# Masking each bank of attention scores by itself, with mask tiles of 64 by 64, in an attention and expert kernel

## What is computed

```python
Q = x @ W_q + b_q; K = x @ W_k + b_k; V = x @ W_v + b_v
scores = jnp.einsum('bhqd,bhkd->bhqk', Qh, Kh)
scores = (scores + jnp.einsum('bhqd,qkd->bhqk', Qh, rel_k)) / scale
scores = jnp.where(causal[None, None], scores, -1000000000.0)
attn = jax.nn.softmax(scores, axis=-1)
out = jnp.einsum('bhqk,bhkd->bhqd', attn, Vh) + jnp.einsum('bhqk,qkd->bhqd', attn, rel_v)
x = x + _layernorm(out @ W_o + b_o)
x = x + _layernorm(ffn(_layernorm(x)))
```

## Time and profile before

| what | value |
|---|---|
| runs | 1043.07, 1037.00, 1040.29 us; median 1040.29 |
| the profiled execution | 1038.87 us, its span in the trace 1037.1 us |
| PE busy | 907.4 us, 87% |
| DVE busy | 834.9 us, 80% |
| POOL busy | 726.3 us, 70% |
| ACT busy | 678.6 us, 65% |
| mask products (L1537) | 1280 matmuls, 199.3 us recorded |
| score products for the maxima (L1516) | 1024 matmuls, 215.5 us |
| score products for the exponentials (L1493) | 1024 matmuls, 196.3 us |
| maxima on DVE (L1127) | 640, 409.3 us |

### The profile page before, as it was taken

One profiled execution on the slowest core, in us unless ns is written; L12 is line 12 of the kernel. 1 busy time (PEld: TensorE's weight loads), 2 busy tenths in 40 slices (PEclk: granted clock), 3 DMA queues, 4 the chain that ended last, 5 costly groups with the idle time before them and its releaser, 6 DMA issues. The chain is left out here.

```text
span 1037.1 us, 23478 instructions
## 1 busy us (share of the span) xinstructions
PE 907.4 (87%) x7655; PEld 519.9 (50%) x7655; DVE 834.9 (80%) x1948; ACT 678.6 (65%) x1305; POOL 726.3 (70%) x940
## 2 busy tenths in 40 slices
PE   2768899999999899999998999987679999999995
PEld 0324444444444444454444444432357777777773
DVE  5677878888888888888888888886568788878884
ACT  2137677767786777777867776765447767676763
POOL 4135676966867868668678686576257989898886
PEclk8569999999999999999999999998979999999999
DMA  2610111101101101011011010102415454554541
GB/s 50 168 45 28 37 39 34 51 33 41 46 32 45 43 33 48 31 43 47 32 45 43 32 49 32 42 13 57 149 58 169 143 165 151 171 148 167 162 139 31
DMA packets 64004, 74.93 MB, mean 72 GB/s; under 512 B 10032, under 2 KB 39600, under 8 KB 63904
## 3 DMA queue, kind: packets, MB, share of 16 engines
q1 hardware_dynamic: 61536, 73.17, 22.2%
q10 hardware_dynamic: 2368, 0.48, 0.3%
HBM read 43.75 MB, written 8.65 MB: 51 GB/s over the span
## 5 line engine op out<-in xcount | busy, mean ns | idle before, releaser
L1127 DVE TENSOR_REDUCE mx<-ps_s 128x1 f32<-128x512 f32 (+2 forms) x640 | 409.3, 684 | 82.3 <-PE ps_s L1537 80.5
L799 ACT ACTIVATE prob<-ps_e 128x512 f32<-128x512 f32 x640 | 347.8, 601 | 121.6 <-PE ps_e L1493 121.6
L640 POOL TENSOR_SCALAR_AFFINE_SELECT prob<-prob 128x516 f32<-128x516 f32 (+1 forms) x320 | 174.0, 568 | 171.3 <-ACT prob L799 171.3
L1516 PE MATMUL ps_s<-ks,qs 63*128 63x512 f16 (+3 forms) x1024 | 215.5, 311 | 20.6 <-DMA ks<-kl 8.6
L1493 PE MATMUL ps_e<-qs,ks 64*128 64x512 f16 (+3 forms) x1024 | 196.3, 304 | 15.8 <-DMA qs<-mT 7.8
L1553 PE MATMUL ps_av<-prob,vp 128*32 128x512 f32 (+3 forms) x2048 | 183.8, 455 | 22.7 <-POOL prob L640 22.4
L721 POOL TENSOR_TENSOR hidden_low<-hidden,hidden_high 128x512 fp32r<-128x512 f32 x144 | 191.2, 1356 | 12.1 <-ACT hidden_high L988 10.8
L1493 PEld LDWEIGHTS ps_e<-qs,ks 64*128 64x128 f16 x1024 | 60.9, 95 | 116.8 <-ACT prob L799 63.9
L988 ACT CAST hidden_high<-hidden 128x512 fp32r<-128x512 f32 x160 | 98.3, 614 | 30.4 <-DVE hidden L1440 25.8
L1537 PE MATMUL ps_s<-masked_at,below_r 64*128 64x130 bf16 (+3 forms) x640 | 106.5, 211 | 0.0
L1516 PEld LDWEIGHTS ps_s<-ks,qs 63*128 63x128 f16 x1024 | 63.6, 95 | 78.0 <-DVE mx L1127 54.5
(11 more groups left out here) (176 smaller groups left out, 1738.4 us busy)
## 6 DMA issues: line engine op xcount, KB each, us to landing
gate_rows<-gates_dram SPq DMA_DIRECT2D x128, 256.0 KB, 3.6
qs<-qh SPq DMA_DIRECT2D x128, 32.0 KB
qs<-ql SPq DMA_DIRECT2D x128, 32.0 KB
xnT_dram<-oT SPq DMA_DIRECT2D x16, 256.0 KB, 2.0
xeT<-xnT_dram SPq DMA_DIRECT2D x16, 256.0 KB, 2.7
out<-result SPq DMA_DIRECT2D x16, 256.0 KB, 2.3
v_near<-v_back SPq DMA_DIRECT2D x16, 254.0 KB
ks<-kh SPq DMA_DIRECT2D x124, 32.0 KB
```

What stands on the lines that cost most here:

```text
L640: pool.affine_select(out=v, in_=v, compare_op=ALU.is_ge, fill=0.0, base=-2, pattern=cols, channel_multiplier=-1).then_inc(S["p_masked"], 1)
L799: act.activation(prob[g % 2][:, u, b, :], ps_e[bank][:, :], ACT.Exp, scale=SCALE).then_inc(S["e_done"], 1)
L1127: dve.tensor_reduce(out, src, AX.X, ALU.max).then_inc(s_free[bank], 1)
L1516: pe.matmul(scores[:, at:at + P * (qt + 1)], qs[par][rows, 2 * g + off, P * qt:P * qt + P], ks[par][rows, 2 * g + off, 0:P * (qt + 1)], st ...
```

## The change

- `s_mask` replaces `diagonals` and `s_masks`. It masks one bank and one half of the queries: `part` chooses queries 0 to 63 or 64 to 127 of each block, and the weights are `below[rows, rows]`, 64 rows by 64 columns, a tile of 64 by 64. Part 1 moves 65 columns per block, as before; part 0 masks the rest and moves 129 columns for one block, 257 for two neighbouring ones and 258 for two of 256 keys. There are still two masks per bank and four per round. The half that must not be touched is masked at once for all of its keys, so `below_r` is not needed.
- `below_r` and `roll_halves` (two copies on ACT and a wait on PE) are gone. `masked_at` grows from 65 to 257 columns and is made by six selects on POOL instead of four.
- `exp_unit` and `s_unit` are cut into bank and part (`e_unit`, `e_part`), so that a round can alternate single products of the two halves. Each bank is masked, and signals `s_full`, when its own products are through: the upper one in the middle of the round, the lower one at the end.
- The number of instructions on PE stays the same. On PE the shape of consecutive tiles changes more often, as the order below shows.

The diff (whole):

```diff
--- before
+++ after
@@ -234,8 +234,7 @@
         ident = sb("ident", [P, P])
         ident16 = sb("ident16", [P, P], F16)
         below = sb("below", [P, P], BF16)
-        below_r = sb("below_r", [P, P], BF16)
-        masked_at = sb("masked_at", [P, HALF + 1], BF16)
+        masked_at = sb("masked_at", [P, 2 * P + 1], BF16)
         head_sel = sb("head_sel", [P, D, NPAIR, 2])
         head_sum = sb("head_sum", [P, 32])
         wq_in = sb("wq_in", [P, P])
@@ -378,7 +377,7 @@
 
 
         names = """
-            attn_loaded qk_loaded x_loaded0 x_loaded1 x_loaded2 const_made const_ready rolled bias_full bias_ready
+            attn_loaded qk_loaded x_loaded0 x_loaded1 x_loaded2 const_made const_ready bias_full bias_ready
             m_made masked_made v_rows k_rows q_rows
             dve_own pool_own gate_own dve_own2 pool_own2 passed_sp passed_pool passed_dve passed_pe
             s_full s_free0 s_free1 s_free2 e_full e_done misc_full misc_free
@@ -596,13 +595,17 @@
 
             def masked_columns():
 
-                for i, (base, columns) in enumerate(((0, slice(0, HALF)), (-HALF, slice(0, HALF)),
-                                                     (1 - HALF, slice(HALF, HALF + 1)), (1 - P, slice(HALF, HALF + 1)))):
-                    v = masked_at[:, columns]
-                    pool.affine_select(out=v, in_=v, compare_op=ALU.not_equal, fill=MASKED, base=base,
-                                       pattern=[[-1 if i < 2 else 0, v.shape[1]]],
-                                       channel_multiplier=1).then_inc(S["masked_made"], 1)
-                    pool.wait_ge(S["masked_made"], i + 1)
+                blocks = masked_at[:, 1:].rearrange("p (n c) -> p n c", n=2)
+                parts = ((masked_at[:, 0:1], 0, [[0, 1]]),
+                         (blocks[:, :, 0:HALF - 1], 1, [[0, 2], [-1, HALF - 1]]),
+                         (blocks[:, :, HALF - 1:], HALF - 1, [[0, 2], [0, HALF + 1]]))
+                made = 0
+                for v, row, pattern in parts:
+                    for b in range(2):
+                        pool.affine_select(out=v, in_=v, compare_op=ALU.not_equal, fill=MASKED, base=-row - HALF * b,
+                                           pattern=pattern, channel_multiplier=1).then_inc(S["masked_made"], 1)
+                        made += 1
+                        pool.wait_ge(S["masked_made"], made)
 
             def selectors():
 
@@ -782,12 +785,6 @@
                         act.dma_start(ks0[lo:lo + D, 0:NPAIR // 2, :],
                                       part[HALF * b:HALF * b + 32, :]).then_inc(stacks[0][0], 16)
 
-            def roll_halves():
-
-                act.wait_ge(S["const_ready"], N_POOL_CONST)
-                act.copy(below_r[0:HALF, :], below[HALF:P, :]).then_inc(S["rolled"], 1)
-                act.copy(below_r[HALF:P, :], below[0:HALF, :]).then_inc(S["rolled"], 1)
-
             def exp_unit(st, i):
                 g, u, b = i // (2 * NU), i % (2 * NU) // 2, i % 2
                 n, bank = st.e_use(f"e{i}")
@@ -906,8 +903,6 @@
                     act.wait_ge(S["gates_stored"], 32)
                     rest = (NSEQ - EARLY) * NE * NT
                     act.copy(gate_sb[0:rest, 0, :], ps_misc[0:rest, 0:P]).then_inc(S["gateT_copied"], 1)
-
-            roll_halves()
 
             def step(st):
                 def exps(lo, hi):
@@ -1482,17 +1477,21 @@
                 need(pe, S["misc_free"], st.misc(what))
                 return ps_misc
 
-            def exp_unit(st, i):
-                g, u, b = i // (2 * NU), i % (2 * NU) // 2, i % 2
-                par, rows = st.b % 2, slice(HALF * b, HALF * b + HALF)
+            def e_unit(st, i):
                 scores = e_bank(st, f"e{i}")
                 if i % HALF_UNITS == 0:
                     pe.wait_ge(mrow[i // HALF_UNITS], st.at(32 * (st.b + 1), 32))
-                for off, kt, at in E_UNITS[u]:
-                    pr = 2 * g + off
-                    last = pe.matmul(scores[:, at:at + WIDTH[kt]], ks[par][rows, pr, P * kt:P * kt + P],
-                                     qs[par][rows, pr, P * kt:SEQ], start=True, stop=True)
-                last.then_inc(S["e_full"], 1)
+                return scores
+
+            def e_part(st, i, scores, n):
+                g, u, b = i // (2 * NU), i % (2 * NU) // 2, i % 2
+                par, rows = st.b % 2, slice(HALF * b, HALF * b + HALF)
+                off, kt, at = E_UNITS[u][n]
+                pr = 2 * g + off
+                last = pe.matmul(scores[:, at:at + WIDTH[kt]], ks[par][rows, pr, P * kt:P * kt + P],
+                                 qs[par][rows, pr, P * kt:SEQ], start=True, stop=True)
+                if n == len(E_UNITS[u]) - 1:
+                    last.then_inc(S["e_full"], 1)
 
             def s_unit(st, i):
 
@@ -1504,9 +1503,7 @@
 
                     pe.wait_ge(S["k_rows"], st.a + 1)
                     pe.wait_ge(S["q_rows"], st.a + 1)
-                scores = s_bank(st, f"s{i}")
-                s_part(st, i, scores, 0)
-                return scores
+                return s_bank(st, f"s{i}")
 
             def s_part(st, i, scores, n):
 
@@ -1516,28 +1513,23 @@
                 pe.matmul(scores[:, at:at + P * (qt + 1)], qs[par][rows, 2 * g + off, P * qt:P * qt + P],
                           ks[par][rows, 2 * g + off, 0:P * (qt + 1)], start=(n == 0), stop=False)
 
-            def diagonals(bank, u, part):
+            def s_mask(u, b, bank, part):
 
                 n = len(S_UNITS[u])
                 apart = SEQ // 2 if u == 2 else P
-                if part == 0 and u != 2:
-                    blocks = bank[:, SEQ - 1 - n * P:SEQ - 1].rearrange("p (n c) -> p n c", n=n)
-                    return blocks[:, :, 0:HALF]
-                blocks = bank[:, SEQ - n * apart:SEQ].rearrange("p (n c) -> p n c", n=n)
-                at = apart - HALF - 1 if part else apart - P - 1
-                return blocks[:, :, at:at + HALF + part]
-
-            def s_masks(u, both):
-
-                n = len(S_UNITS[u])
-                for part in range(2):
-                    for b in (1, 0):
-                        rows = slice(HALF * b, HALF * b + HALF)
-                        columns = masked_at[rows, 0:HALF + part].unsqueeze(1).to_broadcast([HALF, n, HALF + part])
-                        last = pe.matmul(diagonals(both[b], u, part), (below if b == part else below_r)[rows, :],
-                                         columns, start=False, stop=(part == 1))
-                        if part == 1:
-                            last.then_inc(S["s_full"], 1)
+                rows, queries = slice(HALF * b, HALF * b + HALF), slice(HALF * part, HALF * part + HALF)
+                blocks = bank[queries, SEQ - n * apart:SEQ].rearrange("p (n c) -> p n c", n=n)
+                if part:
+                    out = blocks[:, :, apart - HALF - 1:]
+                    columns = masked_at[rows, 0:HALF + 1].unsqueeze(1).to_broadcast([HALF, n, HALF + 1])
+                elif u == 2:
+                    out = blocks[:, :, apart - P - 1:]
+                    columns = masked_at[rows, 0:P + 1].unsqueeze(1).to_broadcast([HALF, n, P + 1])
+                else:
+                    out, columns = bank[queries, SEQ - n * P - 1:SEQ], masked_at[rows, 0:n * P + 1]
+                last = pe.matmul(out, below[rows, rows], columns, start=False, stop=True)
+                if part == 0:
+                    last.then_inc(S["s_full"], 1)
 
             def av_part(st, s, g, kt):
                 par = s % 2
@@ -1735,8 +1727,7 @@
                         "xn2": lambda: xn2_transpose(st), "logits": lambda: logits(st)}
                 if st.t0 == 1:
                     pe.wait_ge(S["const_ready"], N_CONST)
-                    pe.wait_ge(S["rolled"], 2)
-                    pe.wait_ge(S["masked_made"], 4)
+                    pe.wait_ge(S["masked_made"], 6)
 
                     pe.matmul(ps_av[:, 0:P], bias_v[:, :], wo[:, :], start=True, stop=True).then_inc(S["bias_full"], 1)
                 if st.t0 == 2:
@@ -1751,20 +1742,35 @@
                             if st.t0 == NSEQ + 2 and what == "xn2":
                                 first_units(st)
                             use()
-                    both = [None, None]
-
+                    n = len(S_UNITS[u])
+                    if st.A:
+                        upper = s_unit(st, 2 * r)
+                        s_part(st, 2 * r, upper, 0)
                     if st.B:
-                        exp_unit(st, 2 * r)
+                        exps = e_unit(st, 2 * r)
+                        e_part(st, 2 * r, exps, 0)
+                    if st.A and n > 1:
+                        s_part(st, 2 * r, upper, 1)
+                    if st.B and n > 1:
+                        e_part(st, 2 * r, exps, 1)
                     if st.A:
-                        both[1] = s_unit(st, 2 * r)
+                        s_mask(u, 1, upper, 1)
+                        lower = s_unit(st, 2 * r + 1)
```

(19 more changed lines are left out.)

## The result

The changed kernel takes 1449.43 us (median of four runs, 1427.68 to 1477.30), the kernel before 1041.68. It is slower by a factor of **1.374, 95% interval 1.369 to 1.379**; two of its four runs, 1470 and 1477 us, had a lower granted clock still (0.76 against 0.79 and 0.82) and are left out of that ratio. The forecast was 1290 us with a range of 1215 to 1360: the direction was right, the size was not.

What follows compares the result with a forecast made beforehand. PE was taken as the fullest engine, DVE close behind. Per step 41.3 + 18.2 - 4 + 2.2 = 57.7 us; fifteen such steps (246) and 5 for the maxima-only step, on 1038.87, gave 1290 us, range 1215 to 1360.

Steps and rivals of the forecast that it cites:

- The price of a change: On PE in attention: each change of tile shape costs 0.095 us; 127 more per step make 12.1 us.
- part 2: PE's attention rounds: masks stream alone, rounds take 1.44 and 1.80 us; +18.2 us per step, shape changes included.
- part 3: PE's waits in an attention step: the added work fills them, so 4 of 6 us vanish, bounds 0 and 6.
- part 4: PE's clock in attention: three half-clock stretches per step, +2.2 us, bounds 0 and 5.
- The sum: A step with maxima and exponentials takes 57.7 us, +16.4; in all 251 us are added, giving 1290 us.
- Mixed shapes run freely: Rival for PE's attention rounds: 64x128 and 64x64 tiles run side by side, nothing lost; 1010 us, chance 0.04.
- a change inside the same row halves is cheap: Rival on PE's shape changes: they cost say a third, so +8 us per step, 1170 us; chance 0.06.
- The waits stay and the clock falls often: Rival for the attention step: all 6 us of waits stay, clock costs 5 us; 64.5 us, 1390 in all, chance 0.15.
- part 5: Setup of constants: two ACT copies fewer, POOL selects some 0.7 us longer, both hidden; booked as nothing.

Runs made afterwards that it cites:

- tiny64_4: The kernel before plus four matmuls of one zero column per round in 64x64 tiles, between products and masks: 1298.04 us, ratio 1.248.
- wide_tile: The changed kernel with mask weights widened by zero columns, so the tile is 64x128 again, same order: 1038.66 us, ratio 0.998 to the kernel before.
- four_together: The changed kernel's 64x64 masks, all four at the end of a round, products in the order of before: 1062.73 us, ratio 1.020 to the kernel before.
- bank_pairs: The changed kernel with the two 64x64 masks of a bank together behind that bank's products: 1081.16 us, ratio 1.037 to the kernel before.
- values_in_two_places: The old mask products in the new order, with a group's value products in two places instead of three: 1050.95 us, ratio 1.010 to the kernel before.
- twice: The changed kernel with every exponentials product and the first product of each maxima bank done twice: 1569.91 us, ratio 1.509 to the kernel before.

## Why the prediction was right and where it failed

- **The price of a change** (0.095 us) held for a pair of shapes that no row had shown: 0.10 us behind a product, 0.10 per change in tiny64_4. The weight load of a 64x64 mask, taken at 0.02 us, comes out at 0.02 to 0.03 in the timeline, near the upper end of its bound.
- **The round** (part 2) was forecast to 0.01 us: 1.44 and 1.80 against 1.45 and 1.81. wide_tile shows that nothing but the shape makes it; tiny64_4 shows the price of the change without mask columns.
- **The waits** (part 3): I let 4 of 6 us vanish; by 41.3 + 18.2 - 54.6 it was 4.9, and the weight loads' waits for other engines went from 9.6 to 1.2 us.
- **The clock** (part 4) is the step that failed. It put down three stretches of 3.4 us per step at 0.75 us each, 2.2 us, bounds 0 and 5. Measured are 30.6 us per step at half clock, three times as much, and 0.39 us for each instead of the 0.22 (0.75/3.4) that I carried over: 12 us. The 0.22 comes from a stretch in a kernel with waits, in which a slower PE partly only waited less (2.48 of 3.41 us busy, then all of 3.42); with PE as the bound there is no such cushion. The runs bear this out in the main: by the step rows above a microsecond at half clock costs 0.26 us in four_together and 0.40 in bank_pairs, which has hardly a wait left. But values_in_two_places has waits and pays about 0.43 (42.05 to 43.54 us for one fall), so it also matters where in the step the fall lies. And I took the length of a fall, 3.4 us, from the kernel before; in the changed kernel one lasts 41. Why they last so long is open. The step with one fall in values_in_two_places:

```profile
424.50:468.04 43.54, 37.66 (x413) 19.76 (x409) 35.98 (x91) 30.77 (x60) 30.55 (x45) 0.96 0.11 39
```

- **The sum.** With 9.8 us more for the clock and 0.9 us less wait in each of fifteen steps it is 1290 + 147 - 13 = 1424 us, against 1428 in the profiled execution. The range missed because its upper end, 1360, was built with 3 us of clock and 1 us of wait, inside the bounds of 5 and 0 that parts 4 and 3 had set; and even with 5 and 0 it would have stopped near 1390. The FFN stage is as long as before: 293.7 us from its first product to the end in both kernels.
- **The rivals.** "Mixed shapes run freely" and "a change inside the same row halves is cheap" are refuted by the timeline and by tiny64_4. "The waits stay and the clock falls often", 1390 us, was right in its second half and wrong in its first; its own bound for the clock, 5 us, was too low as well. The sign for it that I had named, a granted clock under 0.85, came up. The order's own gain is real but small: 0.6%.
- **The constants** (part 5) cost nothing visible: the first query projection starts at 12.36 instead of 12.20.

## What to carry to other kernels

Count how often the tile shape changes on TensorE, as one counts instructions: each change left nothing streaming for 0.09 to 0.12 us here (the most behind the small tile, with its weight load), and where a lone matmul stands between two changes it also ends what ran side by side. Put small matmuls into the shape of their neighbours, with zero columns in the weights if need be (wide_tile), or group those of another shape. Before crowding PE with such holes, allow for its clock: read what a microsecond at half clock costs where PE is the bound, not in a kernel that still has waits, and do not take the length of a fall from a kernel that recovers at once. A first bank handed over early, in an unchanged shape, was worth 0.4%, and the whole new order 0.6%.

## What the runs showed of the hardware that was not expected

- PE was recorded busy for 866.03 of 866.06 us in the thirteen steady steps, and its granted clock was 0.77. The Trainium skill advises, on the page TensorE: Matmul & The Clock Gate (Why this matters for your kernels), to keep TensorE busy and to avoid idle gaps between bursts; here there was hardly a recorded gap, and the clock fell all the same, so the record's busy share gave no warning. The number of changes alone does not order it either: tiny64_4, with 144 added changes per step, has 0.88 in the step shown, the changed kernel with 127 has 0.67 to 0.89, and bank_pairs with 63 has 0.96 to 1.00.
- Steps of one program differ by a quarter for the clock alone: 59.7 and 73.5 us next to each other, 67.9 and 85.0 in twice.
- A change of the tile's columns alone (32 to 128 on all rows, 128 to 64 on half of them) costs as much as one of its rows.
